# Scores from the values' matmul, and key splitting and one slot's mixing placed between the ranking tiles

## What is computed

```python
normed = _ln(hidden_states, g1, b1)
scores = jax.nn.sigmoid(jnp.einsum('bld,d->bl', normed, Wr) + br)
k = max(1, int(round(ROUTE_FRAC * l)))            # 154 of 1024
_, idx = jax.lax.top_k(-scores, k)                # the lowest scores are attended
q  = (normed @ Wq + bq).reshape(b, l, H, dh)
kk = (normed @ Wk + bk).reshape(b, l, H, dh)
v  = (normed @ Wv + bv).reshape(b, l, H, dh)
...
```

## Time and profile before

| | us |
|---|---|
| median of 3 runs | 1895.57 |
| lowest, highest | 1887.01, 1904.9 |
| the profiled execution, its own time | 1903.3 |
| its span, first to last instruction | 1901.6 |
| PE busy | 1640.8 (86%) |
| DVE busy | 1287.5 (68%) |
| ACT busy | 998.3 (53%) |

### The profile page before, as it was taken

How to read it: one execution, slowest core, us unless ns; L and a number is a source line. 1 busy time by engine, 2 the same in 40 slices (tenths; PEclk the granted TensorE clock), 3 DMA queues, 4 the chain that set the end, 5 groups by cost and what they waited for, 6 DMA issues and landing times.

```text
span 1901.6 us, 26442 instructions
## 1 busy us (share of the span) xinstructions
PE 1640.8 (86%) x9799; PEld 921.1 (48%) x9799; DVE 1287.5 (68%) x3010; ACT 998.3 (53%) x1417; POOL 124.9 (7%) x159
## 2 busy tenths in 40 slices
PE   4789878998999999995476987889899999999935
PEld 2458556663333333363244674756524333333814
DVE  7738643046889999836967577421489899996478
ACT  2432542134777777753542335331457777777345
POOL 6010000000000000004301000000000000000020
PEclk9878896998999999996687698789989999999957
DMA  6021300015001000000000322000430010000001
GB/s 156 0 69 57 82 26 1 1 58 174 26 26 34 26 26 26 9 1 24 27 17 1 117 49 68 1 1 1 133 108 26 27 34 26 26 26 1 1 1 34
DMA packets 53861, 73.39 MB, mean 39 GB/s; under 512 B 18647, under 2 KB 27172, under 8 KB 53734
## 3 DMA queue, kind: packets, MB, share of 16 engines
...
## 4 chain that ended last, share of the span: by engine, by line
PE 69%; DVE 19%; ACT 5%; issue 3%; DMA 2%; POOL 1%; SPq 1%; DVEq 0%; ACTq 0%; POOLq 0%
PE PV L909 10%; PE ST L893 9%; PE S L859 7%; PE ST L805 4%; PE ST L560 3%; PE MT L859 3%; PE ST L590 3%; DVE nmp L1585 2%; PE PV L918 2%; PE S L816 2%; DVE st L1458 2%; DVE amax L1693 2%; DVE R L1692 2%; PE S L854 1%; DVE Er L1513 1%
## 5 line engine op out<-in xcount | busy, mean ns | idle before, releaser
L1257 ACT ACTIVATE Er<-ST 128x1024 f32<-128x1024 f32 x384 | 377.1, 1021 | 105.9 <-PE ST L893 105.6
L1637 DVE TENSOR_REDUCE nmp<-S 128x1 f32<-128x512 f32 x514 | 337.6, 683 | 30.6 <-PE S L859 30.6
L893 PE MATMUL ST<-QS,KS 100*128 100x512 bf16 x768 | 218.0, 385 | 0.3
L909 PE MATMUL PV<-Er,V 128*17 128x512 f32 x1536 | 211.9, 601 | 0.0
L859 PE MATMUL S<-KS,QS 96*128 96x512 bf16 x514 | 183.3, 392 | 2.2 <-DMA QS<-scr_q 1.4
L1637 DVE TENSOR_REDUCE nmp<-MT 128x1 f32<-128x512 f32 x254 | 173.5, 683 | 13.5 <-PE MT L859 13.5
L859 PEld LDWEIGHTS S<-KS,QS 96*128 96x128 bf16 x514 | 48.2, 98 | 156.3 <-DVE nmp L1637 103.3
L448 POOL TENSOR_SCALAR tp<-mv 128x8 f32<-128x8 f32 x20 | 5.5, 275 | 1660.5 <-DVE mv L1462 1660.5
L1585 DVE TENSOR_REDUCE nmp<-S 128x1 f32<-128x512 f32 x120 | 77.6, 684 | 46.3 <-PE S L675 45.9
L893 PEld LDWEIGHTS ST<-QS,KS 100*128 100x128 bf16 x768 | 72.2, 99 | 64.3 <-ACT Er L1257 5.7
L859 PE MATMUL MT<-KS,QS 96*128 96x512 bf16 x254 | 99.4, 391 | 0.9 <-DVE nmp L1637 0.9
...
## 6 DMA issues: line engine op xcount, KB each, us to landing
...
```

What stands on the lines that cost most here:

```text
L893: ins = nc.tensor.matmul(ST[i % 2][:, (kt % 2) * HALF:(kt % 2 + 1) * HALF], KS[0:KP + 4, k, kt * P:(kt + 1) * P], QS[0:KP + 4, k, half * H ...
L909: ins = nc.tensor.matmul(PV[row:row + VC, :], slots[h // H].V[:, kt, h % H, :], E[:, step % RING, (kt % 2) * HALF:(kt % 2 + 1) * HALF], st ...
L1257: A_(E[:, g, :], ST[i % 2][:, :], ACT.Exp).then_inc(s["exps"], 1)
L1637: v.tensor_reduce(nmp[:, u // 2, u % 2:u % 2 + 1], bank, AX.X, ALU.max).then_inc(s["reduced"], 1)
```

## The change

The vector `Wr` becomes column 193 of the values' weights (`wvr`), so that each tile's values and its score logit come out of the same matmuls, and `logits` is gone. ACT takes exp of two logits from each of the four values pieces ahead of copying the piece. Values now come first, straight behind the transposition of each slot, then the score rows, and the keys after them. The sum of the scores is made by DVE (`scsum`) and one matmul, in place of eight.

On DVE the ranking calls `beside(t)` after each tile. Between the last four tiles of slot a stand the cut steps of its keys, and after tile 2 the scores of slot z. Between the tiles of slot z stand the cut steps of z's keys, after tile 2 the pooling and mixing of slot a, and after tile 6 the cut of a's queries. On PE and ACT `premix` and `precopy` of slot a come ahead of `pick` of slot z. SP's and POOL's code is unchanged. The core of the diff, with leading blanks cut:

```diff
@@ -109,10 +109,10 @@
...
-        wr = sb("wr", [CH + 1, 2, 1])
...
-        wv = sb("wv", [CH + 1, 2, D])
+        wvr = sb("wvr", [CH + 1, 2, D + 1])
+        wv = wvr[:, :, 0:D]
@@ -218,6 +218,7 @@
...
+ o.scsum = sb("scsum" + nx, [P, 1])
@@ -253,7 +254,7 @@
...
-        names = """early rest wprep qones loaded consts tokens outproj h1 logit expz score srow_turned srow_copied picks rank_turned rank_copied premixed precopied pt gathersel nts
+        names = """early rest wprep qones loaded consts tokens outproj h1 expz score srow_turned srow_copied picks rank_turned rank_copied premixed precopied pt gathersel nts
@@ -319,8 +320,8 @@
...
- load(wr[0:CH, :, 0], A["L0_ffn_Wr"].rearrange("(c p) -> p c", p=CH))
- load(wr[CH:CH + 1, 1, :], A["L0_ffn_br"].rearrange("(a n) -> a n", a=1))
+ load(wvr[0:CH, :, D], A["L0_ffn_Wr"].rearrange("(c p) -> p c", p=CH))
+ load(wvr[CH:CH + 1, 1, D:D + 1], A["L0_ffn_br"].rearrange("(a n) -> a n", a=1))
@@ -567,16 +568,17 @@
...
+     n = (D + 1, D)[use]
      if use == 0:
-         pe.wait_ge(s["srow_copied"], at(p, o, 1, 1))
+         evacuated(p, o, 1)
...
              for c in range(2):
...
-                 ins = nc.tensor.matmul(banks[i % 2][:, (t % 2) * D:(t % 2 + 1) * D], o.XT[0:r, c, t * P:(t + 1) * P],
-                                        w[0:r, c, off:off + D], start=c == 0, stop=c == 1)
+                 ins = nc.tensor.matmul(banks[i % 2][:, (t % 2) * n:(t % 2 + 1) * n], o.XT[0:r, c, t * P:(t + 1) * P],
+                                        w[0:r, c, off:off + n], start=c == 0, stop=c == 1)
@@ -602,26 +604,24 @@
...
- def logits(p, o):
-     evacuated(p, o, 1)
-     for t in range(T):
-         for c in range(2):
-             r = CH + c
-             ins = nc.tensor.matmul(o.O[:, t:t + 1], o.XT[0:r, c, t * P:(t + 1) * P], wr[0:r, c, :], start=c == 0, stop=c == 1)
-     ins.then_inc(s["logit"], 1)
-     project(p, o, 0, wk, 0, o.XT, HALF, 2)
+ def keys0(p, o, c):
+     pe.wait_ge(s["srow_copied"], at(p, o, 1, 1))
+     project(p, o, 2 * c, wk, 0, o.XT, HALF, 2, (c,))
...
  def scores_row(p, o):
...
-     pe.wait_ge(o.s["resid"], p * 14 + 4)
+     pe.wait_ge(o.s["vcopied"], p * 8 + 4)
...
-     for j in range(3):
+ def pooled(p, o):
+     for j in range(2):
          for t in range(T):
-             lhs = o.X[:, t, j * CH:(j + 1) * CH] if j < 2 else ones[:, 0:CH]
-             ins = nc.tensor.matmul(o.O[0:CH, 16 + j:17 + j], lhs, o.sc[:, t:t + 1], start=t == 0, stop=t == T - 1)
-     ins.then_inc(s["pooled"], 1)
+             nc.tensor.matmul(o.O[0:CH, 16 + j:17 + j], o.X[:, t, j * CH:(j + 1) * CH], o.sc[:, t:t + 1], start=t == 0, stop=t == T - 1)
+     nc.tensor.matmul(o.O[0:CH, 18:19], ones[:, 0:CH], o.scsum[:], start=True, stop=True).then_inc(s["pooled"], 1)
@@ -633,7 +633,6 @@
...
  def queries0(p, o):
...
-     pe.wait_ge(o.s["vcopied"], p * 8 + 4)
@@ -1043,18 +1042,21 @@
...
      for o in slots:
...
-     for o in slots:
-         turn_norm(p, o, 1)
-     for o in slots:
-         logits(p, o)
-     for o in slots:
-         scores_row(p, o)
-     for o in slots:
-         values(p, o, 0, wv, 0)
+     turn_norm(p, a, 1)
+     values(p, a, 0, wvr, 0)
+     turn_norm(p, z, 1)
+     scores_row(p, a)
+     values(p, z, 0, wvr, 0)
+     keys0(p, a, 0)
+     scores_row(p, z)
+     keys0(p, a, 1)
+     keys0(p, z, 0)
+     pooled(p, a)
+     keys0(p, z, 1)
+     pooled(p, z)
...
-     for o in slots:
@@ -1144,7 +1146,7 @@
...
- def cut(p, o, group, pieces, width):
+ def cut(p, o, group, pieces, width, after_two=None):
@@ -1152,6 +1154,8 @@
...
+         if i == group + 1 and after_two is not None:
+             after_two()
@@ -1173,9 +1177,15 @@
...
  def vcopy(p, o, use):
...
+     n = (D + 1, D)[use]
      for i in range(4):
...
-         A_(o.V[:, 2 * i:2 * i + 2, :, 0:DH], banks[i % 2][:, 0:2 * D].rearrange("p (t h d) -> p t h d", t=2, h=H), ACT.Copy).then_inc(o.s["vcopied"], 1)
+         src = banks[i % 2][:, 0:2 * n].rearrange("p (t n) -> p t n", t=2)
+         if use == 0:
+             ins = A_(o.sc1[:, 2 * i:2 * i + 2], src[:, :, D], ACT.Exp, scale=-1.0)
+             if i == 3:
+                 ins.then_inc(s["expz"], 1)
+         A_(o.V[:, 2 * i:2 * i + 2, :, 0:DH], src[:, :, 0:D].rearrange("p t (h d) -> p t h d", h=H), ACT.Copy).then_inc(o.s["vcopied"], 1)
@@ -1310,24 +1320,22 @@
...
-     for o in slots:
-         evac(p, o, 1, o.XT, 2, 3)
-     for o in slots:
-         act.wait_ge(s["logit"], at(p, o, 1, 1))
-         A_(o.sc1[:], o.O[:, 0:T], ACT.Exp, scale=-1.0).then_inc(s["expz"], 1)
-         cut(p, o, 0, pieces_k0(o), HALF)
-     for o in slots:
+     def score_row(o):
...
-     for o in slots:
-         vcopy(p, o, 0)
+     evac(p, a, 1, a.XT, 2, 3)
+     vcopy(p, a, 0)
+     evac(p, z, 1, z.XT, 2, 3)
+     score_row(a)
+     vcopy(p, z, 0)
+     cut(p, a, 0, pieces_k0(a), HALF, lambda: score_row(z))
+     cut(p, z, 0, pieces_k0(z), HALF)
...
          for c in range(2):
...
-     for o in slots:
...
-     for o in slots:
@@ -1507,7 +1515,31 @@
...
- def rank_tokens(p, o):
+ def cut_step(p, o, group, pieces, width, n):
+     i = group + n
+     if n == 0:
+         if o is z:
+             ve.wait_ge(a.s["lo"], p * 14 + group + len(pieces))
+         elif p or group:
+             ve.wait_ge(z.s["lo"], p * 14 + group)
+     if n < len(pieces):
+         ve.wait_ge(o.s["hi"], p * 14 + i + (2 if o is a else 1))
+         if i >= 2:
+             ve.wait_ge(o.s["lo"], p * 14 + i - 1)
+         v.tensor_tensor(R1[:, i % 2, 0:width], o.R2[i % 2][0:CH, 0:width], pieces[n][:, 0, :], ALU.subtract).then_inc(o.s["resid"], 1)
+     if n > 0:
+         ve.wait_ge(o.s["mid"], p * 14 + i)
+         v.tensor_tensor(pieces[n - 1][:, 2, :], R1[:, (i - 1) % 2, 0:width], pieces[n - 1][:, 1, :], ALU.subtract).then_inc(o.s["lo"], 1)
+ def score(p, o):
+     ve.wait_ge(s["expz"], at(p, o, 1, 1))
+     link(v.tensor_scalar(o.sc1[:], o.sc1[:], 1.0, None, ALU.add))
+     link(v.reciprocal(o.sc[:], o.sc1[:]))
+     v.tensor_reduce(o.scsum[:], o.sc[:], AX.X, ALU.add).then_inc(s["score"], 1)
+     ve.wait_ge(s["score"], at(p, o, 1, 1))
+ def rank_tokens(p, o, beside):
@@ -1515,6 +1547,7 @@
...
+         beside(t)
@@ -1749,19 +1782,30 @@
...
      for o in slots:
...
-     for o in slots:
-         ve.wait_ge(s["expz"], at(p, o, 1, 1))
-         link(v.tensor_scalar(o.sc1[:], o.sc1[:], 1.0, None, ALU.add))
-         v.reciprocal(o.sc[:], o.sc1[:]).then_inc(s["score"], 1)
-         ve.wait_ge(s["score"], at(p, o, 1, 1))
-         cut(p, o, 0, pieces_k0(o), HALF)
-     for o in slots:
-         rank_tokens(p, o)
-         pool_tokens(p, o)
-     for o in slots:
-         mix_in(p, o)
-     for o in slots:
-         cut(p, o, 4, pieces_q0(o), 2 * QP)
+     def beside_a(t):
+         if t == 2:
+             score(p, z)
+         if t >= 4:
+             cut_step(p, a, 0, pieces_k0(a), HALF, t - 4)
+     def beside_z(t):
+         if t in (0, 1, 3, 4, 5):
+             cut_step(p, z, 0, pieces_k0(z), HALF, (0, 1, None, 2, 3, 4)[t])
+         if t == 2:
+             pool_tokens(p, a)
+             mix_in(p, a)
+         if t == 6:
+             cut(p, a, 4, pieces_q0(a), 2 * QP)
+     score(p, a)
+     rank_tokens(p, a, beside_a)
+     cut_step(p, a, 0, pieces_k0(a), HALF, 4)
+     rank_tokens(p, z, beside_z)
+     pool_tokens(p, z)
+     mix_in(p, z)
+     cut(p, z, 4, pieces_q0(z), 2 * QP)
```

## The result

| | us |
|---|---|
| changed kernel, median of 4 runs | 1867.51 (1865.64 to 1872.74) |
| kernel before, same chip, 4 runs | 1899.09 (1887.01 to 1904.9) |
| ratio, 95% interval | 0.9844 (0.981 to 0.9879) |
| profiled execution of the changed kernel, its span | 1866.93, 1865.1 |

The changed kernel is some 30 us faster.

What follows compares the result with a forecast made beforehand. DVE was to bound the ranking stage: 7.4 + 5.4 + 47.6 + 2.0 + 13.9 = 76.3 us after a's last evacuation, saving 24.7 over two pairs, so the median 1895.6 becomes 1870.9, range 1860 to 1890.

Steps and rivals of the forecast that it cites:

- Values of a: Value matmuls of slot a, now on the path after a's last evacuation: 7.4 us, bounds 5.3 and 9.0.
- Transposes of z and the score row: PE transposes z and turns a's score row, ACT copies it, before ranking: 5.4 us, between about 4.9 and 5.6.
- DVE's sum: DVE's work from the start of a's ranking to z's selection matrix, the new bottleneck: 47.6 us.
- Waits inside it: DVE's waits for PE and ACT during the ranking stretch: together 2 us, between 0 and 4.6.
- 0 to 3.4 for the queries: DVE's wait for a's queries from PE, during z's ranking: 0 to 3.4 us, taken as 1.
- Nothing for the keys: No DVE waiting counted for key pieces, since ranking tiles of 1.7 us and more stand between the subtractions.
- rival of waiting for key pieces: Inserted cut steps make DVE's ranking wait, up to 2.29 us each, eight a pair: 1880 to 1907 us, chance 0.10.
- Tail: End of the stage: pick, scaling, queries and premix of z, turn of both ranks; 13.9 us, premix of a hidden.
- SP's queue: Loads of a's heads 4 to 7 come 2 to 3 us later against the stage's end, but hidden.
- sign of being wrong, L674 waiting for a load: The first work of `selected` waiting for a load was listed as showing the forecast wrong.
- first L674 of pair 1: Start of `selected` in pair 1, expected at about 1110 as a sign that the forecast is right.
- rival of PE at the lower level: PE runs at its lower clock level where it is on the path: 1876 to 1889 us, chance 0.22.

Runs made afterwards that it cites:

- e1: Changed kernel with four more 128x1024 comparisons on DVE in the ranking of slot z; 1877.06 us, ratio to before 0.9906.
- e6: Changed kernel with the sum of the scores made by eight matmuls again and DVE's reduction gone; 1868.79 us, ratio to before 0.9837.
- e7: Changed kernel with a's score row turned and copied ahead of z's transposition on PE and ACT; 1864.4 us, ratio to before 0.9833.
- e10: Changed kernel with eight more subtractions a pair on GpSimd, on tensors nothing else uses; 1873.87 us, ratio to before 0.9894.
- e2: Changed kernel with both slots' key parts cut on DVE in blocks between the two rankings, none between tiles; 1895.4 us, ratio to before 1.0001.
- e3: Changed kernel with premix and precopy of slot a after pick and queries of slot z again; 1881.57 us, ratio to before 0.9927.
- e4: Changed kernel with 16 one-column logit matmuls a slot put back ahead of the values, result unused; 1896.28 us, ratio to before 1.0004.

## Why the prediction held, and where it was off

Forecast 1870.9, range 1860 to 1890; measured 1867.51. The picture of the stage was right: DVE became its bound (e1), fed by PE from a microsecond or so ahead (e6). The terms, in pair 1 of the changed kernel:

- *Values of a:* 7.4, measured 7.3 (7.7 in pair 0). The choice between 5.3 and 9.0 by the nearest row was right here; e7 and e10 had 8.95 in one pair each, with the same work ahead.
- *Transposes of z and the score row:* 5.4, measured 4.7 (12.0 less 7.3). The transposes ran at a granted clock of 1.00, so my lower bound of 4.9 applied, and was 0.2 too high in this pair.
- *DVE's sum:* 47.6, measured 47.2 with the one wait of 0.2 in it.
- *Waits inside it:* 2.0, between 0 and 4.6; measured 0 but for 0.2. **This is the term that was mis-sized.** z's scores were there in time, and so were a's queries, although the pick of a took 6.13. That this term was 0 is in part luck: PE was 0.8 us ahead at the queries, and in e6 3.3 us more on PE gave 2.2 of waiting. My 0 to 3.4 for the queries had the right place; the middle of it was not what happened.
- *Nothing for the keys:* right, as DVE waited for none. Its cover is worth more than I thought: without the tiles between (e2) DVE's stretch is 13.5 and 13.2 longer. The rival of waiting for key pieces was priced at 2.29 a step; the real waits in e2 were up to 5.44, since a starved PE comes late with several pieces in a row and runs them at the lower level.
- *Tail:* 13.9, measured 13.7, with premix of a hidden as said; e3 prices it at 6.6 to 8.1.
- *SP's queue:* no dearer than before, but not hidden as I had it. PE waits in `selected` for loads of queries and keys, 2.4 and 3.5 us in the two pairs of the changed kernel, and it did so before, 3.7 and 2.9. `selected` took 74.1 and 75.9 against 75.4 and 74.2. So my sign of being wrong, L674 waiting for a load, was badly chosen: the kernel before shows it too.

So the stage is 73.6 and 73.0 in place of 76.3: 30.8 us gained over two pairs against the first profile of before, where I had 24.7. Against both profiles of before and both of the changed kernel (stages of 176.7 and 146.6 in the mean, from the table) it is 30.1, and the medians differ by 31.6 and 33.7. Measured by the gain the forecast was 7 to 9 us too low. That its end point of 1870.9 lies so near 1867.5 is partly luck: it set out from a median of 1895.6, and the kernel before was measured at 1899.1 beside the changed one.

The first L674 of pair 1 came at 1098.0 and not at 1110: 6.0 us from the two stages and 7.9 by mix in pair 0, with 2.2 given back elsewhere, 1.4 of it ahead of the first stage. I had said that all later stages take as long as now; by code they do, but a stretch of them can differ by 8 us from one execution to the next, which a forecast from one profile can't see.

The rival of PE at the lower level was wrong for this kernel: the clock is 0.89 in DVE's stretch, in place of 0.78 and 0.75 in the old first two parts, and 1.00 in the tail as before; where it is low, in the pick of a, PE is off the path. The Trainium skill's page weighed there, "TensorE: Matmul & The Clock Gate", section "Part 1: The HAM clock gate (the "warmup" mystery)", names idle gaps as what brings the lower level back. Both sides mattered. Narrow matmuls stayed at 0.50 with PE fully busy (e4), and where an experiment made a gap of 6 to 9 us, the dense work behind it was slow (e2, e3). In the changed kernel the longest gap, 3.3 us, came where DVE had other work.

How much each part is worth, by what the stage loses without it, for a pair: logits on their own again 13.3 to 13.4, the steps between tiles 15.4 to 15.8, premix of a between the picks 6.5 to 8.1, the one matmul for the sum of scores 2.0 to 2.1. The sum is far above the gain of 15.4 a pair: they overlap, and can't be added. No run puts PE's old order back, with keys ahead of the score row, and nothing else; that the order is what moves the ranking forward by the remaining 16 to 17 us is read from e4's row, and not from a run of its own.
